# State-space front of a decoder kernel: parts of delta cast on ScalarE, first two scan steps from 32-row products, stacked copies counted by quarter

## The chip, the cores and the metric

One NeuronCore of one Trainium2 chip runs the whole kernel. The metric is the device time of one launch in microseconds, the median of three runs. Smaller is better.

## The reference, cut to the stage that is touched

The program is a decoder of two layers over x of shape (2, 256, 128), with a context of (2, 512, 128). The change is in the first block, a gated selective state-space model (the first 74 us or so); two cross-attentions, a self-attention and two expert feed-forward blocks follow it. What the block computes:

```python
def _selective_ssm(x, dt_w, dt_b, Bp_w, Bp_b, Cp_w, Cp_b, A_log, D_p):
    delta = jax.nn.softplus(x @ dt_w + dt_b)
    Bt = x @ Bp_w + Bp_b
    Ct = x @ Cp_w + Cp_b
    A = -jnp.exp(A_log)                       # (128, 16)
    def step(h, inp):
        xt, dt, bt, ct = inp
        dA = jnp.exp(dt[..., None] * A)
        dBx = dt[..., None] * bt[:, None, :] * xt[..., None]
        h = dA * h + dBx
        y = jnp.einsum('bdn,bn->bd', h, ct)
        return (h, y)
...
xn = _ln(x, ln1_g, ln1_b); xm = _ln(xn, ln_g, ln_b)
x1 = xm @ w1_w + w1_b
xc = silu(conv1d(x1, conv_w, width 3, per channel))
y = _selective_ssm(xc, ...)
v = silu(xm @ v1_w + v1_b)
x = (y * v) @ w2_w + w2_b + res
```

The matmul and convolution lines of the second half are abridged; the first function is as it stands.

## The kernel before, in words

Five engine programs (TensorE, VectorE, ScalarE, GpSimd and SyncE, which issues all DMAs) are written out by hand, each in a fixed order, and meet at semaphores. Nothing is scheduled by a tool: an engine runs its instructions in the order of the code, and an instruction whose semaphore has not come holds back all behind it.

**The front.** Two norms on VectorE (with GpSimd for the reciprocal roots), four transposes on TensorE, the projections w1 and v1, the convolution on VectorE, two Silu on ScalarE (`gate`, then `xc`), then three projections of `xc` into PSUM banks 3, 4 and 5: dt, B and C. delta is softplus: ScalarE does Abs, Exp and Ln into `dtmp`, VectorE puts it together as `dl[:, 0]` (L960). ScalarE also forms `nA` = -exp(A_log) (L662, L664), and copies B and C out of PSUM (L673, L675) and the normed context `cxnT` (L641, two of them). A change of function set on ScalarE costs a table load, which stands as a row of its own; `set_table` (L647) is a one-column activation that draws the load to its place.

**The spread.** The scan runs with 128 lanes that hold 8 channels by 16 states, so there are 16 scan steps `s`, each over all 512 tokens. Step s needs eight channels of delta, each repeated over 16 lanes, and the same of delta times xc (called dx). The repetition is a matmul with a 0/1 selector `sel_g`. To keep float32 accuracy from bf16 products, delta and dx are each split into three bf16 parts (`dparts`, three parts of each of the two kinds): part 0 is the cast, part 1 the cast of the rest, part 2 what is then left. A product sums the three parts at once, because they are stacked on 96 rows in `quads[32 * part + row, kind, q]`, where q = 0 to 3 is the quarter of 32 channels. Moving a part to its row group crosses partitions. For q = 0 ScalarE does it for delta (three copies, L684) and VectorE for dx (three copies, L971); for q = 1, 2 and 3 SyncE issues 18 DMAs from SBUF to SBUF (L445), each of 32 KB. `ORDER` gives quarter and index of each step: (0,0), (0,1), (1,0), (1,1), (2,0), (3,0), (2,1), (3,1), and then (q, 2) and (q, 3) for all four q.

**A scan step.** TensorE spreads delta into bank s % 2 and dx into bank 2 + s % 2; ScalarE does exp(scale * delta) with the scale from `nA` into `dA` (L708); VectorE multiplies the dx bank by B (L978) and scans (L983); GpSimd multiplies by C (L544). Beside each step TensorE does four products of the value projection of the next attention (`values0`), and ScalarE copies those out (L699). TensorE may write the banks of step s when `dA_done` and `scan_done` have reached s - 1. Step 2 waits for the six copies of q = 1 (`second_quads`), step 4 for the twelve copies of q = 2 and 3 together (`late_quads`).

## Time and profile before

| | |
|---|---|
| median of 3 runs | 488.54 us (488.38 to 488.86) |
| profiled execution, its own time | 487.24 us |
| its span (first to last instruction) | 485.1 us |
| TensorE busy, of the span | 423.2 us, 87% |
| VectorE / ScalarE / GpSimd busy | 306.9 / 206.8 / 145.0 us |
| mean granted TensorE clock | 0.976 of full |
| first scan step's multiply (L978) | starts at 32.09 us |
| last scan ends | about 63.6 us |

The profile is of one execution; its times count from the span's start. A busy share says little here, since the stages have different limits: the front is a chain through four engines, the scan stage is VectorE's, the rest is mostly TensorE's. So what a change in the front is worth is read from the chain of the front and from what each scan step waited for.

### The profile page before, as it was taken

The numbers are of one execution on the slowest core, as the hardware profiler recorded it, in microseconds if no ns is written. First come the engines' busy times: TensorE is split into PE (matmuls) and PEld (weight loads), VectorE is DVE, ScalarE is ACT, GpSimd is POOL, SyncE is SP. The second block draws the span as 40 slices with busy tenths as digits, with TensorE's granted clock in tenths as the row PEclk, the third lists the DMA queues.
The fourth block names the chain that finished last, engine by engine and source line by source line (L and its number), as shares of the span: only waits on it lengthen the run. The fifth ranks groups of instructions, "written<-read, shape, count | busy, mean of one in ns | idle before, by whom it ended". The sixth has DMA issues, their size and how long they took to land.

```text
span 485.1 us, 7466 instructions
## 1 busy us (share of the span) xinstructions
PE 423.2 (87%) x2852; PEld 269.4 (56%) x2860; DVE 306.9 (63%) x712; ACT 206.8 (43%) x268; POOL 145.0 (30%) x138
## 2 busy tenths in 40 slices
PE   5867989999999999789999878698578999997984
PEld 5665645444555556556778355344434445556874
DVE  4789976676666665416213587953697777338754
ACT  1765623333333322153323388574154445546320
POOL 3226647877777774100302200000200000005111
PEclk9989999999999999999999887999998999999998
DMA  8611000000023110610440430000000000010000
GB/s 306 263 34 59 1 0 2 1 1 1 0 84 134 45 45 0 219 51 1 110 59 17 62 40 3 3 3 1 0 1 3 1 3 1 2 34 1 1 1 22
DMA packets 7791, 19.58 MB, mean 40 GB/s; under 512 B 1862, under 2 KB 3686, under 8 KB 7238
## 3 DMA queue, kind: packets, MB, share of 16 engines
q1 hardware_dynamic: 7756, 19.10, 13.5%
q8 instruction: 23, 0.38, 0.3%
q14 instruction: 12, 0.10, 0.1%
HBM read 17.26 MB, written 1.15 MB: 38 GB/s over the span
## 4 chain that ended last, share of the span: by engine, by line
PE 60%; DVE 21%; ACT 5%; issue 5%; POOL 5%; SPq 2%; DMA 1%; DVEq 0%; POOLq 0%
PE ps L1373 58%; DVE ps L1170 3%; DVE mx_a L1174 2%; POOL big L588 2%; SPq L445 1%; ACT big L768 1%; DVE big L983 1%; DVE ps L978 1%; POOL rstd L521 1%; PE ps L1385 1%; POOL big L595 1%; PE ps L1753 1%; DMA ident<-in_ident 1%; DVE big L1332 1%; DVE attn_w L917 1%
## 5 line engine op out<-in xcount | busy, mean ns | idle before, releaser
L1373 PE MATMUL ps<-big,late 128*32 128x256 f32 (+4 forms) x792 | 99.8, 383 | 11.8 <-DVE mid L909 4.5
L1373 PEld LDWEIGHTS ps<-big,late 128*32 128x32 f32 (+3 forms) x800 | 38.9, 117 | 52.0 <-issue 22.0
L794 ACT ACTIVATE big<-ps 128x1024 f32<-128x1024 f32 x48 | 48.9, 1023 | 40.3 <-PE ps L1373 39.8
L1373 PE MATMUL ps<-late,big 128*128 128x128 f32 (+1 forms) x448 | 64.1, 275 | 1.6 <-DVE mx_x L1170 1.3
L519 POOL TENSOR_SCALAR vareps<-meanvar 128x4 f32<-128x4 f32 (+2 forms) x11 | 2.6, 232 | 197.4 <-DVE meanvar L886 193.7
L732 ACT ACTIVATE big<-ps 128x1024 f32<-128x1024 f32 x32 | 32.8, 1024 | 65.3 <-PE ps L1373 58.9
L1373 PEld LDWEIGHTS ps<-late,big 128*128 128x128 f32 (+1 forms) x448 | 44.7, 152 | 25.2 <-issue 21.0
L588 POOL TENSOR_TENSOR big<-big 128x512 f32<-128x512 f32 x32 | 41.0, 1283 | 28.2 <-DVE big L1055 28.2
L1170 DVE CUSTOM_DVE_ANT_0 ps<-ps,big 128x512 f32<-128x512 f32 x64 | 42.6, 717 | 10.0 <-PE ps L1373 6.9
L1055 DVE TENSOR_SCALAR big<-big 128x1024 f32<-128x1024 f32 x32 | 27.6, 864 | 33.3 <-ACT big L732 33.3
L1373 PE MATMUL ps<-ident 128*128 128x128 f32 x232 | 30.3, 293 | 5.7 <-DMA ident<-in_ident 5.7
L1373 PEld LDWEIGHTS ps<-ident 128*128 128x128 f32 x232 | 29.5, 209 | 6.8 <-DMA ident<-in_ident 5.7
L1373 PE MATMUL ps<-ctx_r,attn_w 128*128 128x512 f32 x64 | 32.6, 619 | 0.7 <-ACT late L699 0.7
L753 ACT ACTIVATE big<-ps 128x512 f32<-128x512 f32 x32 | 18.9, 597 | 29.0 <-PE ps L1373 29.0
L1373 PE MATMUL ps<-attn_w,big 128*128 128x128 f32 x192 | 25.9, 281 | 6.0 <-DVE big L1332 3.7
L1373 PE MATMUL ps<-xT,late 128*128 128x512 f32 x64 | 29.0, 596 | 1.2 <-ACT big L753 1.2
L1373 PEld LDWEIGHTS ps<-attn_w,big 128*128 128x128 f32 x192 | 23.4, 192 | 10.0 <-DVE big L1332 5.3
L1046 DVE RECIPROCAL big<-ps 128x256 f32<-128x256 f32 x16 | 28.0, 1748 | 1.3 <-PE ps L1373 1.3
L1096 DVE SCALAR_TENSOR_TENSOR summed<-ps,g,summed 128x128 f32<-128x128 f32 x28 | 7.9, 344 | 31.5 <-PE ps L1373 31.5
L1373 PE MATMUL ps<-big,mid 64*128 64x256 f32 x192 | 27.2, 403 | 0.0
L1373 PE MATMUL ps<-xT,attn_w 128*128 128x256 f32 (+1 forms) x80 | 24.8, 433 | 0.9 <-ACT xT L641 0.9
L544 POOL TENSOR_TENSOR big<-big,mid 128x512 f32<-128x512 f32 x16 | 20.4, 1272 | 16.2 <-DVE big L983 16.2
(255 smaller groups left out, 691.8 us busy)
## 6 DMA issues: line engine op xcount, KB each, us to landing
attn_w<-in_w_x SPq DMA_DIRECT2D x1, 2560.0 KB, 13.1
big<-parts_kx SPq DMA_DIRECT2D x18, 128.0 KB
late<-in_w_up SPq DMA_DIRECT2D x1, 2048.0 KB, 8.9
late<-in_w_dn SPq DMA_DIRECT2D x4, 512.0 KB, 3.9
attn_w<-in_w_up SPq DMA_DIRECT2D x1, 1024.0 KB, 5.9
attn_w<-in_w_dn SPq DMA_DIRECT2D x1, 1024.0 KB, 7.9
parts_kx<-ctx_r SPq DMA_DIRECT2D x1, 768.0 KB, 3.3
rowv<-in_rowv SPq DMA_DIRECT2D x1, 576.0 KB, 4.1
```

The lines of the kernel that those rows point to most:

```text
L445: sp.dma_start(quads[32 * i:32 * i + 32, kind, q, :], dparts[32 * q:32 * q + 32, kind, i, :]).then_inc(S["second_quads" if q == 1 else "la ...
L544: nc.gpsimd.tensor_tensor(hC[:, s % 8, :], hs[:, s % 4, :], Cn[:], ALU.mult).then_inc(S["hC_done"], 1)
L588: nc.gpsimd.tensor_tensor(esum[:, s, :].rearrange("p (r t) -> p r t", r=2), e[:, :, 0, :], e[:, :, 1, :], ALU.add).then_inc(S["e0_sum"], 1)
L732: nc.scalar.activation(ex[:, n % 3, :].rearrange("p (r n) -> p r n", r=2), ps[:, 2 * (n % 2):2 * (n % 2) + 2, :], ACT.Exp).then_inc(S["e0_ ...
L753: nc.scalar.activation(eh0[:, e % 2, c, :], ps[:, n % 3, :], ACT.Gelu).then_inc(S["up0_act"], 1)
L794: nc.scalar.activation(ex1[:, n % 3, :].rearrange("p (r n) -> p r n", r=2), ps[:, 2 * (n % 2):2 * (n % 2) + 2, :], ACT.Exp, scale=scale).t ...
L1046: link(nc.vector.reciprocal(dst, ps[:, 4 + b, T:2 * T]))
L1055: nc.vector.tensor_scalar(ex[:, n % 3, :], ex[:, n % 3, :], float(np.exp(CLIP)), float(np.exp(-CLIP)), ALU.min, ALU.max).then_inc(S["e0_cl ...
L1096: ins = nc.vector.scalar_tensor_tensor(summed[:, j, :], ps[:, 5 + e % 2, j * D:(j + 1) * D], g0[:, 3, j, e:e + 1], summed[:, j, :] if e el ...
L1170: nc.vector.tensor_tensor_reduce(ps[:, bank, :], ps[:, bank, :], mq[:, 2 * b + q, :], 1.0, -FAR, ALU.add, ALU.max, dst).then_inc(S[f"{L}_r ...
L1174: nc.vector.tensor_reduce(dst, ps[:, bank, :].rearrange("p (h k) -> p h k", h=heads), AX.X, ALU.max).then_inc(S[f"{L}_redmax"], 1)
L1373: return nc.tensor.matmul(o, lhsT, rhs, start=start, stop=stop, skip_group_check=shared)
```

## The change

Five things are done, all in the front of the first block:

- `nA` is made at the very start of ScalarE's program, in place of the one-column Identity. Where it stood, ahead of Abs, there is now a `set_table(ACT.Exp)`.
- Parts 0 and 1 of delta are cast by ScalarE (behind the copy of B and the copy of C), part 2 is subtracted by VectorE, not GpSimd. VectorE computes dx before it starts on the rests. ScalarE's table load for Exp and the two `cxnT` copies now come behind the second cast.
- The six copies for q = 0 ahead of step 0 (L684, L971) are gone. Steps 0 and 1 take each part straight from `dparts[0:32]` by a product of 32 rows, three of them accumulated in PSUM (`first_spread`): twelve products in the place of four. `values0(0, 0)` and `values0(0, 1)` both stand behind them.
- SyncE now issues 24 copies, in the order of the list `QUADS`; q = 0, which is needed from step 8 on, comes last.
- Each quarter has a semaphore: steps 2, 4, 5 and 8 wait for q = 1, 2, 3 and 0, with six copies each.

Some semaphores were renamed or merged (`rope_signed`, `x_scr` and `ones_rows`), with the same waits in effect. The diff, without the lists of semaphores and that renaming:

```diff
@@ -321,6 +321,13 @@
+        QUADS = ([(0, 0, 1), (0, 0, 2), (0, 0, 3), (0, 1, 1), (1, 0, 1), (0, 2, 1), (1, 1, 1), (1, 2, 1)]
+                 + [(0, 1, 2), (0, 2, 2)] + [(1, i, 2) for i in range(PARTS)]
+                 + [(0, 1, 3), (0, 2, 3)] + [(1, i, 3) for i in range(PARTS)]
+                 + [(kind, i, 0) for kind in range(2) for i in range(PARTS)])
...
+        QUAD_SEMS = ("first_quads", "second_quads", "late_quads", "third_quads")
...
@@ -438,13 +445,10 @@
-            for q in (1, 2, 3):
-                for kind, parts in enumerate(("delta_parts", "dx_parts")):
-                    for i in range(PARTS):
-                        sp.wait_ge(S[parts], i + 1)
-                        sp.dma_start(quads[32 * i:32 * i + 32, kind, q, :],
-                                     dparts[32 * q:32 * q + 32, kind, i, :]
-                                     ).then_inc(S["second_quads" if q == 1 else "late_quads"], 16)
+            for kind, i, q in QUADS:
+                sp.wait_ge(S["dx_parts" if kind else "delta_parts"], i + 1)
+                sp.dma_start(quads[32 * i:32 * i + 32, kind, q, :], dparts[32 * q:32 * q + 32, kind, i, :]
+                             ).then_inc(S[QUAD_SEMS[q]], 16)
...
@@ -529,10 +533,6 @@
-            pool.wait_ge(S["delta_parts"], 2)
-            nc.gpsimd.tensor_tensor(dparts[:, 0, 2, :], dtmp[:, 0, :], dparts[:, 0, 1, :], ALU.subtract
-                                    ).then_inc(S["delta_parts"], 1)
...
@@ -648,7 +648,9 @@
             act.wait_ge(consts, 1)
-            set_table(ACT.Identity)
+            link(nc.scalar.activation(nA[:, 0, :], vec[:, VEC["A_log"][0]:VEC["A_log"][0] + NG],
+                                      ACT.Exp))
+            link(nc.scalar.mul(nA[:, 1, :], nA[:, 0, :], -1.0))
             to_cols(xT[:], 0, "xT_ps", "xT_done", v("ln_g"), v("ln_b"), 1)
...
@@ -659,9 +661,7 @@
             nc.scalar.activation(xc[:], cv[:, 0, :], ACT.Silu).then_inc(S["xc_done"], 1)
-            link(nc.scalar.activation(nA[:, 0, :], vec[:, VEC["A_log"][0]:VEC["A_log"][0] + NG],
-                                      ACT.Exp))
-            link(nc.scalar.mul(nA[:, 1, :], nA[:, 0, :], -1.0))
+            set_table(ACT.Exp)
             act.wait_ge(S["dt_ps"], 1)
...
@@ -672,18 +672,17 @@
                                  ).then_inc(S["BC_done"], 1)
+            act.wait_ge(S["delta_done"], 1)
+            nc.scalar.activation(dparts[:, 0, 0, :], dl[:, 0, :], ACT.Copy).then_inc(S["delta_parts"], 1)
             nc.scalar.activation(Cn[:], ps[:, 5, :], ACT.Identity, bias=v("Cp_b")
...
+            act.wait_ge(S["delta_rest"], 1)
+            nc.scalar.activation(dparts[:, 0, 1, :], dtmp[:, 0, :], ACT.Copy
+                                 ).then_inc(S["delta_parts"], 1)
+            set_table(ACT.Exp)
             for i in range(2):
...
                         v("ctx_g"), v("ctx_b"), i + 1)
-            set_table(ACT.Exp)
-            act.wait_ge(S["delta_parts"], PARTS)
-            for i in range(PARTS):
-                ins = nc.scalar.activation(quads[32 * i:32 * i + 32, 0, 0, :], dparts[0:32, 0, i, :],
-                                           ACT.Copy)
-            ins.then_inc(S["delta_quads"], 1)
...
@@ -951,25 +950,30 @@
             dve.wait_ge(S["lg_done"], 1)
-            link(nc.vector.scalar_tensor_tensor(dl[:, 0, :], cv[:, 1, :], 0.0, dtmp[:, 2, :],
-                                                ALU.max, ALU.add))
-            nc.vector.tensor_copy(dparts[:, 0, 0, :], dl[:, 0, :]).then_inc(S["delta_parts"], 1)
-            dve.wait_ge(S["delta_parts"], 1)
-            link(nc.vector.tensor_tensor(dtmp[:, 0, :], dl[:, 0, :], dparts[:, 0, 0, :], ALU.subtract))
-            nc.vector.tensor_copy(dparts[:, 0, 1, :], dtmp[:, 0, :]).then_inc(S["delta_parts"], 1)
+            nc.vector.scalar_tensor_tensor(dl[:, 0, :], cv[:, 1, :], 0.0, dtmp[:, 2, :],
+                                           ALU.max, ALU.add).then_inc(S["delta_done"], 1)
+            dve.wait_ge(S["delta_done"], 1)
             dve.wait_ge(S["xc_done"], 1)
             link(nc.vector.tensor_tensor(dl[:, 1, :], dl[:, 0, :], xc[:], ALU.mult))
-            split(dl[:, 1, :], [dparts[:, 1, i, :] for i in range(3)], dtmp[:, 1, :], S["dx_parts"])
-            dve.wait_ge(S["dx_parts"], PARTS)
-            for i in range(PARTS):
-                ins = nc.vector.tensor_copy(quads[32 * i:32 * i + 32, 1, 0, :], dparts[0:32, 1, i, :])
-            ins.then_inc(S["dx_quads"], 1)
+            dve.wait_ge(S["delta_parts"], 1)
+            nc.vector.tensor_tensor(dtmp[:, 0, :], dl[:, 0, :], dparts[:, 0, 0, :], ALU.subtract
+                                    ).then_inc(S["delta_rest"], 1)
+            nc.vector.tensor_copy(dparts[:, 1, 0, :], dl[:, 1, :]).then_inc(S["dx_parts"], 1)
+            dve.wait_ge(S["dx_parts"], 1)
+            link(nc.vector.tensor_tensor(dtmp[:, 1, :], dl[:, 1, :], dparts[:, 1, 0, :], ALU.subtract))
+            dve.wait_ge(S["delta_parts"], 2)
+            dve.wait_ge(S["delta_rest"], 1)
+            nc.vector.tensor_tensor(dparts[:, 0, 2, :], dtmp[:, 0, :], dparts[:, 0, 1, :], ALU.subtract
+                                    ).then_inc(S["delta_parts"], 1)
+            nc.vector.tensor_copy(dparts[:, 1, 1, :], dtmp[:, 1, :]).then_inc(S["dx_parts"], 1)
+            dve.wait_ge(S["dx_parts"], 2)
+            nc.vector.tensor_tensor(dparts[:, 1, 2, :], dtmp[:, 1, :], dparts[:, 1, 1, :], ALU.subtract
+                                    ).then_inc(S["dx_parts"], 1)
...
@@ -1412,7 +1416,6 @@
             pe.wait_ge(ld["sel"], 32)
-            pe.wait_ge(S["delta_parts"], PARTS)
             pe.wait_ge(S["gate_done"], 1)
...
@@ -1443,28 +1446,34 @@
+            def first_spread(kind, s):
...
+                for part in range(PARTS):
+                    pe.wait_ge(S[("delta_parts", "dx_parts")[kind]], part + 1)
+                    ins = mm(ps[:, 2 * kind + s, :], sel_g[0:32, ORDER[s][1], :],
+                             dparts[0:32, kind, part, :], part == 0, part == PARTS - 1)
+                ins.then_inc(S[("spread_d", "spread_x")[kind]], 1)
...
+            first_spread(0, 0)
+            first_spread(0, 1)
+            first_spread(1, 0)
+            first_spread(1, 1)
+            pe.wait_ge(ld["x0"], 16)
+            pe.wait_ge(S["cxnT_done"], 2)
+            values0(0, 0)
+            values0(0, 1)
             for s, (q, i) in enumerate(ORDER):
-                if s >= 2:
-                    pe.wait_ge(S["dA_done"], s - 1)
-                if s == 0:
-                    pe.wait_ge(S["delta_quads"], 1)
-                elif s == 2:
-                    pe.wait_ge(S["second_quads"], 16 * 2 * PARTS)
-                elif s == 4:
-                    pe.wait_ge(S["late_quads"], 16 * 4 * PARTS)
+                if s < 2:
+                    continue
+                pe.wait_ge(S["dA_done"], s - 1)
+                if s in (2, 4, 5, 8):
+                    pe.wait_ge(S[QUAD_SEMS[q]], 16 * 2 * PARTS)
                 mm(ps[:, s % 2, :], sel_g[:, i, :], quads[:, 0, q, :]).then_inc(S["spread_d"], 1)
-                if s == 0:
-                    pe.wait_ge(S["dx_quads"], 1)
-                if s >= 2:
-                    pe.wait_ge(S["scan_done"], s - 1)
+                pe.wait_ge(S["scan_done"], s - 1)
                 mm(ps[:, 2 + s % 2, :], sel_g[:, i, :], quads[:, 1, q, :]
...
                     y_of((7, 9, 14).index(s))
-                if s == 0:
...
-                    pe.wait_ge(ld["x0"], 16)
-                    pe.wait_ge(S["cxnT_done"], 2)
                 values0(s // 2, s % 2)
```

**From Ln to the first scan steps, on ScalarE and VectorE.** ScalarE before: the first row is the Ln (L670), `mid` written from `ps` is B and C, `ctx_r` is `cxnT`, L684 the copies into `quads`, L708 the exponent of steps 0 and 1.

```order
L670 ACTIVATE dtmp<-dtmp 128x512 [waits act_own]
L673 ACTIVATE mid<-ps,vec 128x512 [waits BC_ps]
L675 ACTIVATE mid<-ps,vec 128x512
L641 ACTIVATE ctx_r<-ps,vec 128x512 [waits cxnT_ps] x2
L647 ACT_TABLE_LOAD
L647 ACTIVATE act_table<-neghalf 128x1
L684 ACTIVATE big<-mid 32x512 [waits delta_parts]
L684 ACTIVATE big<-mid 32x512 x2
L708 ACTIVATE big<-ps,nA 128x2x255 [waits spread_d] x2
```

ScalarE now, from the same Ln; L676 and L680 are the casts of delta's parts, L707 the exponent.

```order
L670 ACTIVATE dtmp<-dtmp 128x512 [waits act_own]
L673 ACTIVATE mid<-ps,vec 128x512 [waits BC_ps]
L676 ACTIVATE mid<-mid 128x512 [waits delta_done]
L677 ACTIVATE mid<-ps,vec 128x512
L680 ACTIVATE mid<-dtmp 128x512 [waits delta_rest]
L647 ACT_TABLE_LOAD
L647 ACTIVATE act_table<-neghalf 128x1
L641 ACTIVATE ctx_r<-ps,vec 128x512 [waits cxnT_ps] x2
L707 ACTIVATE big<-ps,nA 128x2x255 [waits spread_d] x2
```

Two casts of 128 partitions have come in, each behind a wait on VectorE, the three copies of 32 partitions are gone, and table load and `cxnT` copies have moved behind the second cast.

VectorE before, from delta (L960) to the multiply of step 0 (L978); L902 to L911 are the split of dx.

```order
L960 SCALAR_TENSOR_TENSOR mid<-cv,dtmp 128x512 [waits lg_done,dve_own]
L962 CAST mid<-mid 128x512 [waits dve_own]
L964 TENSOR_TENSOR dtmp<-mid 128x512 [waits delta_parts]
L965 CAST mid<-dtmp 128x512 [waits dve_own]
L967 TENSOR_TENSOR mid<-mid 128x512 [waits xc_done]
L902 CAST mid<-mid 128x512 [waits dve_own]
L904 TENSOR_TENSOR dtmp<-mid 128x512 [waits dx_parts]
L909 CAST mid<-dtmp 128x512 [waits dve_own]
L911 TENSOR_TENSOR mid<-dtmp,mid 128x512 [waits dx_parts]
L971 COPY big<-mid 32x512 [waits dx_parts]
L971 COPY big<-mid 32x512 x2
L978 TENSOR_TENSOR ps<-ps,mid 128x512 [waits spread_x,BC_done]
```

VectorE now, from delta (L958) to the multiply of step 0 (L982).

```order
L958 SCALAR_TENSOR_TENSOR mid<-cv,dtmp 128x512 [waits lg_done,dve_own]
L962 TENSOR_TENSOR mid<-mid 128x512 [waits xc_done,delta_done]
L964 TENSOR_TENSOR dtmp<-mid 128x512 [waits delta_parts,dve_own]
L966 CAST mid<-mid 128x512
L968 TENSOR_TENSOR dtmp<-mid 128x512 [waits dx_parts]
L971 TENSOR_TENSOR mid<-dtmp,mid 128x512 [waits delta_rest,delta_parts,dve_own]
L973 CAST mid<-dtmp 128x512
L975 TENSOR_TENSOR mid<-dtmp,mid 128x512 [waits dx_parts]
L982 TENSOR_TENSOR ps<-ps,mid 128x512 [waits spread_x,BC_done]
```

Two casts and three copies have left VectorE, one subtraction (L971 now) has come in, and two instructions wait for ScalarE's casts (`delta_parts`).

**The first steps on TensorE.** Before, from the idle products on `ident` to step 2; `big,sel` is a spread, `attn_w,ctx_r` is `values0`.

```order
L1373 MATMUL ps<-ident 128x128 x20
L1373 MATMUL ps<-big,sel 128x512 [waits gate_done,delta_quads,delta_parts,loaded_sel]
L1373 MATMUL ps<-big,sel 128x512 [waits dx_quads]
L1373 MATMUL ps<-attn_w,ctx_r 128x128 [waits cxnT_done,loaded_x0]
L1373 MATMUL ps<-attn_w,ctx_r 128x128 x3
L1373 MATMUL ps<-big,sel 128x512 x2
L1373 MATMUL ps<-attn_w,ctx_r 128x128 x4
L1373 MATMUL ps<-big,sel 128x512 [waits second_quads,dA_done]
L1373 MATMUL ps<-big,sel 128x512 [waits scan_done]
```

Now; `mid,sel` is a product of 32 rows, straight from a part.

```order
L1377 MATMUL ps<-ident 128x128 x20
L1377 MATMUL ps<-mid,sel 128x512 [waits delta_parts,gate_done,loaded_sel]
L1377 MATMUL ps<-mid,sel 128x512 [waits delta_parts] x5
L1377 MATMUL ps<-mid,sel 128x512 [waits dx_parts] x6
L1377 MATMUL ps<-attn_w,ctx_r 128x128 [waits cxnT_done,loaded_x0]
L1377 MATMUL ps<-attn_w,ctx_r 128x128 x7
L1377 MATMUL ps<-big,sel 128x512 [waits second_quads,dA_done]
L1377 MATMUL ps<-big,sel 128x512 [waits scan_done]
```

Twelve products stand where four did, and all eight of `values0` for the first two steps stand behind them.

**SyncE's copies**, before and then now, from the last input load (L438, now L445) to the load of `cxT`.

```order
L438 DMA eb<-in_eb 128x32
L445 DMA big<-mid 32x512 [waits delta_parts] x3
L445 DMA big<-mid 32x512 [waits dx_parts] x3
L445 DMA big<-mid 32x512 [waits delta_parts] x3
L445 DMA big<-mid 32x512 [waits dx_parts] x3
L445 DMA big<-mid 32x512 [waits delta_parts] x3
L445 DMA big<-mid 32x512 [waits dx_parts] x3
L460 DMA ctx_r<-in_cxT 128x1024 [waits cxnT_ps]
```

```order
L445 DMA eb<-in_eb 128x32
L450 DMA big<-mid 32x512 [waits delta_parts] x4
L450 DMA big<-mid 32x512 [waits dx_parts]
L450 DMA big<-mid 32x512 [waits delta_parts]
L450 DMA big<-mid 32x512 [waits dx_parts] x2
L450 DMA big<-mid 32x512 [waits delta_parts] x2
L450 DMA big<-mid 32x512 [waits dx_parts] x3
L450 DMA big<-mid 32x512 [waits delta_parts] x2
L450 DMA big<-mid 32x512 [waits dx_parts] x3
L450 DMA big<-mid 32x512 [waits delta_parts] x3
L450 DMA big<-mid 32x512 [waits dx_parts] x3
L464 DMA ctx_r<-in_cxT 128x1024 [waits cxnT_ps]
```

The first copies of dx stood behind one of delta's third part and came three in a row; now copies of delta's first part for all of q = 1, 2 and 3 lead, and six more stand at the end.

## Rows read from the trace of the kernel before

**Rows 1.** The page, part 4: the chain that ended last, share by engine.

```profile
PE 60%; DVE 21%; ACT 5%; issue 5%; POOL 5%; SPq 2%; DMA 1%; DVEq 0%; POOLq 0%
```

**Rows 2.** The chain in order of time: start us, us, what (SPq is SyncE's queue).

```profile
30.66 0.51 SPq L445
...
37.54 0.59 SPq L445
38.13 0.04 issue
38.17 1.83 DMA big<-mid
```

**Rows 3.** Timeline of VectorE: start us, us, engine, line, operation, tiles, shapes, count, idle before.

```profile
24.48 0.69 DVE L960 SCALAR_TENSOR_TENSOR mid<-cv,dtmp 128x512 f32<-128x512 f32 x1 [1.45 <-ACT dtmp L670]
25.21 0.43 DVE L962 CAST mid<-mid 128x512 bf16<-128x512 f32 x1
25.67 0.69 DVE L964 TENSOR_TENSOR dtmp<-mid 128x512 f32<-128x512 f32 x1
...
27.46 1.26 DVE L902 CAST mid<-mid 128x512 bf16<-128x512 f32 x1
...
30.66 0.87 DVE L971 COPY big<-mid 32x512 bf16<-32x512 bf16 x3
32.09 0.70 DVE L978 TENSOR_TENSOR ps<-ps,mid 128x512 f32<-128x512 f32 x1 [0.56 <-PE ps L1373]
32.83 1.22 DVE L983 TENSOR_TENSOR_SCAN big<-big,ps 128x512 f32<-128x512 f32 x1
34.44 0.70 DVE L978 TENSOR_TENSOR ps<-ps,mid 128x512 f32<-128x512 f32 x1 [0.40 <-PE ps L1373]
...
40.77 0.70 DVE L978 TENSOR_TENSOR ps<-ps,mid 128x512 f32<-128x512 f32 x1 [0.65 <-PE ps L1373]
...
42.64 0.67 DVE L978 TENSOR_TENSOR ps<-ps,mid 128x512 f32<-128x512 f32 x1
...
46.33 0.68 DVE L978 TENSOR_TENSOR ps<-ps,mid 128x512 f32<-128x512 f32 x1
```

**Rows 4.** Timeline of ScalarE, from the table load behind `xc` on.

```profile
19.29 1.28 ACT L662 ACT_TABLE_LOAD   x1
20.59 0.22 ACT L662 ACTIVATE nA<-vec 128x16 f32<-128x16 f32 x1
...
21.08 0.69 ACT L666 ACTIVATE dtmp<-ps,vec 128x512 f32<-128x512 f32 x1
...
23.75 0.63 ACT L670 ACTIVATE dtmp<-dtmp 128x512 f32<-128x512 f32 x1
...
25.42 1.45 ACT L641 ACTIVATE ctx_r<-ps,vec 128x512 f32<-128x512 f32 x2
...
28.46 1.91 ACT L684 ACTIVATE big<-mid 32x512 bf16<-32x512 bf16 x3
```

**Rows 5.** Timeline of GpSimd: the subtraction for delta's third part.

```profile
26.90 1.53 POOL L534 TENSOR_TENSOR mid<-dtmp,mid 128x512 bf16<-128x512 f32 x1 [4.59 <-DVE mid L965]
```

**Rows 6.** Timeline of TensorE: PE is the product, PEld its weight load.

```profile
22.88 4.63 PE L1373 MATMUL ps<-ident 128*128 128x128 f32 x40
30.52 0.38 PE L1373 MATMUL ps<-big,sel 96*128 96x512 bf16 x1 [3.00 <-ACT big L684]
...
31.82 1.73 PE L1373 MATMUL ps<-attn_w,ctx_r 128*128 128x128 f32 x8
...
35.57 0.21 PEld L1373 LDWEIGHTS ps<-big,sel 96*128 96x128 bf16 x2
35.68 0.60 PE L1373 MATMUL ps<-big,sel 96*128 96x512 bf16 x2
...
36.12 1.06 PE L1373 MATMUL ps<-attn_w,ctx_r 128*128 128x128 f32 x8
```

**Rows 7.** Windows: stretch, length, busy us by engine, granted clock, DMA share, GB/s.

```profile
33.00:34.00 1.00, 1.00 (x5) 0.66 (x5) 1.00 (x1) 0.00 (x0) 0.00 (x0) 0.50 0.25 66
288.40:291.80 3.40, 2.88 (x12) 1.47 (x12) 2.13 (x8) 3.30 (x6) 0.00 (x0) 0.50 0.00 0
```

19 lines of the change are left out of this document (9 added, 10 removed).

## The prediction, made before the changed kernel had run

> **What bounds the kernel now.** I first read the chain that ended last by engine: 60% of it is TensorE, 21% VectorE, 5% ScalarE, 2% SyncE's queue [rows 1]. So the kernel as a whole is a TensorE kernel, but a chain's share says nothing of the stage that is touched. I therefore read the chain in order of time over that stage. It runs through ScalarE (Silu, the two operations for `nA`, Abs, Exp, Ln), then through VectorE's splits, and at 30.66 it jumps to SyncE: twelve copies in a row, the last issued at 37.54, then 1.83 us of transfer until 40.00 [rows 2]. Only then can step 4 be spread. The reader should see two things: the end of the front is the queue of copies, and that queue could not go on before the first part of dx, and then ran issue after issue.
>
> Then the timeline of VectorE. Its multiplies of the scan steps start at 32.09, 34.44, then (step 4) 40.77, 42.64 (step 5) and 46.33 (step 7) [rows 3]. From step 4 to 7 that is (46.33 - 40.77) / 3 = 1.85 us a step, VectorE being busy all the time. From step 0 to 4 it is 8.68 us where four such steps are 7.41: 1.27 us of waiting, of which 2.35 - 1.85 = 0.50 lie behind step 0 and the other 0.77 ahead of step 4. Behind step 0 TensorE is slow: its clock is granted at 0.50 in the stretch from 33 to 34, so at 1.2 GHz [rows 7], and eight records of `values0` take 1.73 us where they take 1.06 four microseconds later [rows 6]. Before that TensorE had ended its idle products at 27.51 and had nothing until 30.52 [rows 6].
>
> **The change, part by part.** Times are those of the profiled execution.
>
> *Table and exponent.* Between the table load at 19.29 and Abs at 21.08 stand the two operations for `nA`; the first starts at 20.59, so both cost 0.49 [rows 4]. One small activation, about 0.22 like the first of them, takes their place: 0.27 saved. Abs, Exp, Ln and delta come 0.27 earlier, since ScalarE runs them without a gap. The two operations at the program's start cost nothing: they lie in the wait for the first transposes. There are as many table loads as before. Delta, which ended at 24.48 + 0.69 = 25.17 [rows 3], ends at 24.90.
>
> *Casts on ScalarE.* A cast on VectorE takes 0.43 [rows 3]; ScalarE takes 0.63 for a float32 tile of 128x512 in SBUF [rows 4]. The first cast runs from 24.94 to 25.57, about the 25.64 at which it ended before. It costs 0.2 more and gives the 0.27 back. VectorE does dx meanwhile (0.69), to 25.61, so it hardly waits.
>
> *VectorE up to the last part of dx.* From 25.67, with ScalarE's signal some 0.1 behind: four subtractions at 0.69 and two casts at 0.43 make 3.62, so 29.25. The cast of 27.46 took 1.26 instead of 0.43, beside GpSimd's subtraction from 26.90 to 28.43 [rows 3, 5]; I take it that this 0.83 goes with the GpSimd instruction, as no other lies there. If it stays, the last part comes at 30.1. Before, it came just ahead of the three copies at 30.66, which took 0.87 more [rows 3].
>
> *Twelve products of 32 rows.* A product of 96 rows takes 0.38, a pair 0.60, so each further one costs 0.22 [rows 6]. The trace has none of 32 rows. Bounds: 0.22 from the pair, and 0.44, twice that, were the clock at half. I take 0.22, as rows streamed (512) are what is alike. Delta's third part comes at about 28.15; from there stand seven products up to the one that closes dx of step 0: it starts at 28.22 + 6 x 0.22 = 29.54, behind the last part at 29.25, and ends at 29.92. The multiply of step 0 starts at 29.95, not 32.09: **2.14 us earlier**. At 0.44 each it would be 6 x 0.22 = 1.3 us later, still ahead of before.
>
> The weight loads of a pair overlap it: two of 0.21 in all from 35.57, the products from 35.68 on at 0.22 apart [rows 6], in the same rows of the array. The Trainium skill (TensorE: Matmul & The Clock Gate, The mechanism) says that a load overlaps a running product only where the two use other row groups, and here all twelve use the same. By that rule each of the six gaps ahead of step 0 grows by the load's 0.10, and the first multiply comes 0.6 later, at 30.55, and with the 0.3 that the copies below leave free the time would be 485.7; the trace does not agree for 96 rows.
>
> *ScalarE's second cast, table load, `cxnT`.* The rest of delta is there at 26.36, the cast ends at 27.02, the load 1.28 later, the small activation brings 28.54, the two `cxnT` copies (1.45) 29.97 [rows 4]. The three copies of 1.91 are gone [rows 4]. So the exponent of step 0 runs from 30.0 to 30.7, and the scan of step 0 can start at 30.73, not 32.83 [rows 3]. ScalarE and TensorE arrive within 0.1 us: whichever slips delays the start.
>
> *Steps 1 to 3.* If TensorE has work from 28.2 on, I expect its clock to stay at 2.4 GHz: its gap is then 27.51 to 28.2, not 3 us. `values0` for both steps ends at about 30.2 + 2 x 1.06 = 32.4. Step 2 also needs q = 1. That and step 3 then go at 1.85: **0.50 saved**. With the clock at half, both `values0` take 1.7 and this 0.5 stays.
>
> *The copies.* One issue takes (37.54 - 30.66) / 11 = 0.625 [rows 2]. The first starts at 25.62, as before, and each of the parts is there when its turn comes (the tightest, dx part 2 for the eighth, at 29.25 against 30.0). So the eighth lands at 25.62 + 8 x 0.625 + 1.83 = 32.45, the thirteenth at 35.6, the eighteenth at 38.7, the twenty-fourth at 42.4. Needed: step 2 at about 32.5 (free until 33.2), step 4 at 36.8, step 8 at about 44.6, all met. Step 5's multiply would start at 29.95 + 5 x 1.85 = 39.2; from 38.7 on it needs 0.14 to start and 0.60 for the pair [rows 2, 6], so 39.5. The 0.77 ahead of step 4 goes, **a new wait of 0.3 ahead of step 5 comes**: step 5 stands at 39.5 instead of 42.64, **3.1 us earlier**. SyncE's load of `cxT` behind the copies is used only in layer 1.
>
> Sum: 2.14 + 0.50 + 0.77 - 0.3 = 3.1 us. It has a ceiling of its own: the queue starts when it did before, so a faster front would buy nothing more, and up to 0.3 us of slip there costs nothing. Steps 5 to 15 are VectorE's at 1.85 and wait only for work of their own stage. Behind them the chain is TensorE's, and nothing there waits for a load of the start. I let the 3.1 through whole. The profiled execution would be 487.24 - 3.1 = 484.1 (its span 482.0); it is 1.3 below the median of the runs, and I predict against that: 488.54 - 3.1 = **485.4 us**.
>
> **The rivals.**
>
> *A. The start slips.* Products of 32 rows at 0.44, a half-rate clock in steps 0 to 3, or the 0.83 of the cast staying: each costs 0.5 to 1.0 beyond the slack, together 1.5 at most. Gain 1.6 to 2.6, time 486.0 to 486.9. For it: TensorE now works in thin groups between waits. Against: before, it had been idle for 3 us ahead of the clock's fall [rows 6, 7], and that gap goes. Chance 0.16.
>
> *B. The gain is given back later.* Something behind the scans does not move. For it: over nine tenths of the time are made behind the front. Against: every wait there is on another engine's work, and the chain has no absolute point. Gain under 1, time about 488. Chance 0.07.
>
> *C. Slower.* Later on TensorE's clock is at half in the stretch from 288.4 to 291.8 while it is busy 2.88 of 3.40 us [rows 7]; half of such a stretch, up to 1.7 us, is lost. The clock falls behind waits of TensorE, and the waits stand elsewhere in time if everything shifts by 3 us. The price passes the gain from two further such stretches on (3.4 against 3.1) and is felt as slower with three: 488.54 - 3.1 + 5.1 = 490.5. Against: the three runs of before lie within 0.5 us, so no such thing comes and goes there. Chance 0.05.
>
> *D. More than thought,* 3.8 or more (484.7 or less), if one of the later stretches at half rate vanishes: 1.7 more, 483.7. Chance 0.06.
>
> **How the numbers follow.** The forecast, a gain of 2.6 to 3.7, has 0.66. The range reaches from 484.0 (most of D out) to 487.0, the end of A; B and C are outside, with 0.12, and half of D. 0.2% of this kernel, 1.0 us, is about what a measurement can tell from none: forecast, A and D are faster (0.88), B is the same (0.07), C slower (0.05).
>
> **What would show it.** Right: Abs at about 20.8; two casts of 0.63 on ScalarE; no cast on VectorE over 0.5; step 0's multiply at 29.9 to 30.1 and step 1's 1.85 behind; the clock at 1.00 from 28 to 36; the eighteenth copy landed at 38.7 and step 5's multiply at 39.5 with a wait of 0.3 for it; after that the same intervals as before. Wrong: a start later than 30.6, steps over 1.85 apart among the first four, a copy's landing over 2 us, or a later interval that is longer than before by what the front has gained.

## The result, and the profile after

The changed kernel takes **485.51 us** (median of 21 runs, 483.55 to 490.45); the kernel before, run beside it, 488.77 us (21 runs, 486.98 to 496.43). The ratio is 0.9947, with a 95% interval of 0.9925 to 0.9968, so 2.6 us less, give or take 1.1. The run of 496.43 us is a slow one and is left out of the ratio. The prediction was 485.4 us, range 484.0 to 487.0. The profiled execution of the changed kernel took 486.05 us with a span of 484.2, against 487.24 and 485.1 in the kernel before.

The chain that ended last, by engine, for [rows 1]: SyncE's queue has gone from 2% to 0%.

```profile
PE 63%; DVE 21%; issue 5%; POOL 5%; ACT 4%; DMA 1%; SPq 0%; DVEq 0%; POOLq 0%; ACTq 0%
```

ScalarE's timeline in the changed kernel, for [rows 4]: Abs follows the small activation by 0.11 us, and two casts of 0.63 us stand where VectorE had them.

```profile
18.41 0.63 ACT L663 ACTIVATE mid<-cv 128x512 f32<-128x512 f32 x1 [0.23 <-DVE cv L944]
19.06 1.28 ACT L647 ACT_TABLE_LOAD   x1
20.35 0.20 ACT L647 ACTIVATE act_table<-neghalf 128x1 f32<-128x1 f32 x1
20.46 0.67 ACT L666 ACTIVATE dtmp<-ps,vec 128x512 f32<-128x512 f32 x1
...
24.57 0.63 ACT L676 ACTIVATE mid<-mid 128x512 bf16<-128x512 f32 x1 [0.26 <-DVE mid L958]
...
26.03 0.63 ACT L680 ACTIVATE mid<-dtmp 128x512 bf16<-128x512 f32 x1 [0.25 <-DVE dtmp L964]
...
29.41 1.25 ACT L707 ACTIVATE big<-ps,nA 128x510 f32<-128x510 f32 x2
```

VectorE's timeline, for [rows 3]. The multiplies of the scan's steps are the L982 rows.

```profile
23.85 0.69 DVE L958 SCALAR_TENSOR_TENSOR mid<-cv,dtmp 128x512 f32<-128x512 f32 x1 [1.44 <-ACT dtmp L670]
24.57 0.69 DVE L962 TENSOR_TENSOR mid<-mid 128x512 f32<-128x512 f32 x1
...
25.91 0.42 DVE L966 CAST mid<-mid 128x512 bf16<-128x512 f32 x1
...
28.16 0.69 DVE L975 TENSOR_TENSOR mid<-dtmp,mid 128x512 bf16<-128x512 f32 x1
29.63 0.70 DVE L982 TENSOR_TENSOR ps<-ps,mid 128x512 f32<-128x512 f32 x1 [0.78 <-PE ps L1377]
...
31.50 0.67 DVE L982 TENSOR_TENSOR ps<-ps,mid 128x512 f32<-128x512 f32 x1
...
33.99 0.70 DVE L982 TENSOR_TENSOR ps<-ps,mid 128x512 f32<-128x512 f32 x1 [0.56 <-PE ps L1377]
...
35.86 0.67 DVE L982 TENSOR_TENSOR ps<-ps,mid 128x512 f32<-128x512 f32 x1
...
37.71 0.68 DVE L982 TENSOR_TENSOR ps<-ps,mid 128x512 f32<-128x512 f32 x1
...
39.56 0.68 DVE L982 TENSOR_TENSOR ps<-ps,mid 128x512 f32<-128x512 f32 x1
```

And step 3's multiply in the kernel before, which [rows 3] leaves out:

```profile
38.19 0.67 DVE L978 TENSOR_TENSOR ps<-ps,mid 128x512 f32<-128x512 f32 x1
```

TensorE's timeline and windows (stretch, length, busy us of PE, PEld, DVE, ACT and POOL, granted clock, DMA share, GB/s), for [rows 6, 7], and SyncE's queue.

```profile
22.65 4.63 PE L1377 MATMUL ps<-ident 128*128 128x128 f32 x40
27.21 2.96 PE L1377 MATMUL ps<-mid,sel 32*128 32x512 bf16 x12
30.10 3.00 PE L1377 MATMUL ps<-attn_w,ctx_r 128*128 128x128 f32 x16
32.89 1.06 PE L1377 MATMUL ps<-big,sel 96*128 96x512 bf16 x2
...
37.99 0.59 PE L1377 MATMUL ps<-big,sel 96*128 96x512 bf16 x2 [0.21 <-DMA big<-mid]
```

```profile
30.00:31.00 1.00, 1.00 (x9) 0.90 (x9) 0.97 (x2) 0.67 (x2) 0.00 (x0) 0.99 0.16 42
31.00:34.00 3.00, 3.00 (x15) 2.57 (x14) 2.40 (x4) 1.03 (x2) 1.76 (x2) 0.50 0.19 52
...
195.00:198.00 3.00, 3.00 (x9) 1.97 (x9) 1.71 (x7) 0.07 (x1) 0.00 (x0) 0.50 0.26 68
```

```profile
25.23 15.18 SPq L450 DMA_DIRECT2D big<-mid  x24
```

Step 5's multiply stands at 39.56 instead of 42.64: **3.08 us earlier**. By its parts, each the interval of [rows 3] less that of the rows above: 0.24 because the whole front began earlier in this execution (Silu of `xc` at 18.41); 0.39 between that Silu and the end of delta; 1.83 from the end of delta to the first multiply (5.09 instead of 6.92); 0.48 between steps 0 and 1 (1.87, was 2.35); 0.73 between steps 3 and 4 (37.71 - 35.86, was 40.77 - 38.19); 0.02 between 4 and 5. **And 0.61 lost** between steps 1 and 2: 2.49 where 1.88 was, under a granted clock of 0.50. Together 3.08.

The last scan ends at 60.54, 3.08 before that of the kernel before (63.62). From there to the last instruction the changed kernel's profiled execution takes 2.2 us more. The reader sees where by the start of GpSimd's first operation of each norm (`vareps`), before and after: 200.80 and 198.32, then 267.18 and 265.78, and 481.26 and 480.25 at the end. So 0.60 of the lead is lost up to the first of these norms, 1.08 up to the second and 0.39 behind it. Around the first norm lies a stretch at half rate, from 194.8 to 198.2, that the trace of the kernel before does not have. (It has one from 363.1 to 366.5 that the changed kernel's lacks, and there no lead is won: the interval between the norms on both sides of it is 80.76 us before and 80.75 after.) So this one execution keeps 1.2 of the 3.1 us, and only the medians show the 3.

### The profile page after: what moved, and what is told of

It is laid out like the page before. It is cut to its first block, busy times and chain, and to the rows that moved or that the text cites. A ratio compares the mean times of both kernels' runs of the same rounds, so it can differ in the third digit from the quotient of the medians.

```text
span 484.2 us, 7494 instructions
## 1 busy us (share of the span) xinstructions
PE 426.3 (88%) x2868; PEld 270.2 (56%) x2868; DVE 304.9 (63%) x708; ACT 206.0 (43%) x267; POOL 143.4 (30%) x137
## 4 chain that ended last, share of the span: by engine, by line
PE 63%; DVE 21%; issue 5%; POOL 5%; ACT 4%; DMA 1%; SPq 0%; DVEq 0%; POOLq 0%; ACTq 0%
PE ps L1377 61%; DVE ps L1174 3%; DVE mx_a L1178 2%; DVE big L987 2%; POOL big L588 2%; ACT big L767 1%; DVE ps L982 1%; PE ps L1389 1%; POOL rstd L525 1%; DVE big L1059 1%; POOL big L595 1%; PE ps L1762 1%; DMA ident<-in_ident 1%; DVE big L1336 1%; DVE big L1050 1%
## 5 line engine op out<-in xcount | busy, mean ns | idle before, releaser
L1377 PE MATMUL ps<-big,late 128*32 128x256 f32 (+4 forms) x800 | 101.0, 382 | 11.4 <-DVE mid L908 4.9
L1377 PE MATMUL ps<-xT,attn_w 128*128 128x256 f32 (+1 forms) x80 | 24.8, 433 | 0.9 <-ACT xT L641 0.9
```

The costliest lines, as they stand in the source:

```text
L1377: return nc.tensor.matmul(o, lhsT, rhs, start=start, stop=stop, skip_group_check=shared)
```

## The experiments

Positions in the front are compared from the end of delta, since one execution's front starts later than another's: the Silu of `xc` starts between 18.36 and 19.51. Where several runs are named, the time is their median, and the ratio is that of this kernel to the kernel before on the same chip.

**Copies alone.** The kernel before, with the new order of its 18 copies and own counts by quarter (q = 0 still by ScalarE and VectorE):

```
-for q in (1, 2, 3): for kind, ...: for i in range(PARTS): sp.dma_start(...)
+for kind, i, q in QUADS:            # the changed kernel's order, without q = 0
-elif s == 4: pe.wait_ge(S["late_quads"], 16 * 4 * PARTS)
+elif s in (4, 5): pe.wait_ge(S[QUAD_SEMS[q]], 16 * 2 * PARTS)
```

> The kernel before with one part of the change: the 18 copies in the new order, and steps 2, 4 and 5 each waiting for its own quarter. Front, casts and the copies of q = 0 as before. My sum puts 0.77 us to this part (the wait ahead of step 4): step 0's multiply stays at 32.1, step 5's comes at 41.9 instead of 42.64, time some 0.8 us under the kernel before, ratio 0.9985. Rival (the copies gave most of it, since the queue was the chain's last link): step 5 at 40 and 2 us or more. Rival (all of the gain is the earlier start): no change, step 4 waits as before.

Measured: 488.27 us (10 runs), ratio 0.9999 [0.998, 1.0019]. VectorE's multiplies of steps 3, 4 and 5:

```profile
38.23 0.68 DVE L980 TENSOR_TENSOR ps<-ps,mid 128x512 f32<-128x512 f32 x1
...
40.08 0.68 DVE L980 TENSOR_TENSOR ps<-ps,mid 128x512 f32<-128x512 f32 x1
...
41.93 0.68 DVE L980 TENSOR_TENSOR ps<-ps,mid 128x512 f32<-128x512 f32 x1
```

The wait ahead of step 4 is gone: step 4 follows step 3 by 1.85 instead of 2.58, 0.73 less, for 0.77 predicted. From the end of delta, step 5 comes only 0.42 earlier (17.04 instead of 17.46), because here the clock fell to half at 31.1 and not at 32.0: the first multiply comes 7.14 after delta (6.92 before) and step 1 follows by 2.49 (2.35). The whole time shows no gain; 0.7 us is inside the interval of plus or minus 0.9.

**The wait for both quarters put back** into the changed kernel (step 4 waits for q = 2 and q = 3):

```
-if s in (2, 4, 5, 8): pe.wait_ge(S[QUAD_SEMS[q]], 16 * 2 * PARTS)
+if s in (2, 4, 8):    pe.wait_ge(S[QUAD_SEMS[q]], 16 * 2 * PARTS)
+if s == 4:            pe.wait_ge(S[QUAD_SEMS[3]], 16 * 2 * PARTS)
```

> The changed kernel, but step 4 waits for the copies of q = 2 and of q = 3, as before the change. By my account of the queue the eighteenth copy lands at about 37.85, so step 4's multiply comes at 38.6 instead of 37.71 and step 5's at 40.45 instead of 39.56: 0.9 us of the gain is lost, time about 486.4. Rival (the queue is no limit, counting by quarter did nothing): step 4 and the time unchanged.

Measured: 488.04 us (10 runs), ratio 0.9994 [0.9977, 1.001]. TensorE waits ahead of step 4's pair:

```profile
39.09 0.59 PE L1377 MATMUL ps<-big,sel 96*128 96x512 bf16 x2 [1.55 <-DMA big<-mid]
```

The last scan ends 36.93 us after delta, 36.00 in the changed kernel: 0.93 for the wait, or 0.67 against the changed kernel's second trace below (36.26). The median is 2.5 above the changed kernel's, which was not run beside it; 0.7 to 0.9 of it is this wait, the rest was not located. Both edits to the copies together say that the count by quarter is worth 0.7 to 0.9 us in the front.

**Delta's third part on GpSimd again:**

```
-nc.vector.tensor_tensor(dparts[:, 0, 2, :], dtmp[:, 0, :], dparts[:, 0, 1, :], ALU.subtract)
+nc.gpsimd.tensor_tensor(dparts[:, 0, 2, :], dtmp[:, 0, :], dparts[:, 0, 1, :], ALU.subtract)
```

> The changed kernel with the subtraction for delta's third part on GpSimd again. If VectorE's cast is stretched by GpSimd's instruction, one cast of VectorE between 26.7 and 28.3 takes about 1.26 us instead of 0.42 and delta's third part comes 0.5 later: step 0's multiply at 30.1 instead of 29.63, time 0 to 0.5 us over the changed kernel. Rival (the 1.26 of before was a property of that cast, not of GpSimd): no cast over 0.5, VectorE 0.69 shorter, step 0 no later than 29.7.

Measured: 486.81 us (10 runs), ratio 0.9982 [0.996, 1.0004]. VectorE, and GpSimd's one instruction:

```profile
26.29 0.42 DVE L971 CAST mid<-mid 128x512 bf16<-128x512 f32 x1
26.75 0.69 DVE L973 TENSOR_TENSOR dtmp<-mid 128x512 f32<-128x512 f32 x1
27.48 1.26 DVE L974 CAST mid<-dtmp 128x512 bf16<-128x512 f32 x1
```

```profile
27.18 1.27 POOL L539 TENSOR_TENSOR mid<-dtmp,mid 128x512 bf16<-128x512 f32 x1 [4.72 <-ACT mid L685]
```

The cast that lies beside GpSimd's subtraction takes 1.26, the one ahead of it 0.42; the subtraction on VectorE at 26.75, also partly beside it, keeps its 0.69. The prediction's reading of [rows 3, 5] holds. The first multiply comes 5.38 after delta instead of 5.09: 0.29 later, as delta's third part is (GpSimd ends at 28.45, 3.53 after delta; VectorE's subtraction in the changed kernel ended 3.24 after it). It is no more than that because VectorE is spared the subtraction. The clock stayed full in this trace, and the last scan ends 35.61 after delta, earlier than in the changed kernel (36.00).

**The stack of q = 0 instead of 32-row products** (three copies on ScalarE and three on VectorE, four products of 96 rows, 18 DMAs, all else as changed):

```
-first_spread(0, 0); first_spread(0, 1); first_spread(1, 0); first_spread(1, 1)
+pe.wait_ge(S["delta_parts"], PARTS + 1)
+for s in range(2): mm(ps[:, s, :], sel_g[:, s, :], quads[:, 0, 0, :])
+... (the same for dx), and the six copies into quads[:, :, 0] as before
```

> The changed kernel, but steps 0 and 1 by stacked products of 96 rows: ScalarE (three copies, 1.9 us, ahead of the cxnT copies) and VectorE (three copies, 0.87) fill q = 0, and SyncE issues 18 copies. My account: exponent of step 0 at 31.3 instead of 29.4, scan of step 0 at 32.0 instead of 30.36, step 5's multiply at 40.7 to 41.0 instead of 39.56, time 1.1 to 1.5 us over the changed kernel. Rival (the queue of copies alone sets step 5, and the products of 32 rows bring nothing): step 5 at 39.6 and the time of the changed kernel.

Measured: 487.89 us (10 runs), ratio 0.9985 [0.9965, 1.0006]. TensorE and VectorE:

```profile
30.22 1.86 PE L1386 MATMUL ps<-big,sel 96*128 96x512 bf16 x4 [2.84 <-ACT big L684]
28.98 0.87 DVE L984 COPY big<-mid 32x512 bf16<-32x512 bf16 x3
31.77 0.70 DVE L991 TENSOR_TENSOR ps<-ps,mid 128x512 f32<-128x512 f32 x1 [1.91 <-PE ps L1386]
```

The first multiply comes 7.13 after delta, 2.04 later than with the 32-row products; as the steps behind it then go at 1.85 without a gap, the last scan ends 1.36 later. Step 0's scan starts at 32.50, for 32.0 expected: the granted clock is 0.50 from 29.9 on, behind TensorE's wait of 2.84 us, and the four products take 1.86 us where 0.38 + 3 x 0.22 = 1.04 would do. By an estimate, 0.6 to 0.7 of the 2.04 is this half rate. Without it the multiply would come about 6.5 after delta, only 0.4 earlier than in the kernel before (6.92), although the casts are on ScalarE: TensorE waits for ScalarE's three copies, so the parts of the change do not simply add. The 32-row products are the largest of them.

**The changed kernel a second time:**

> The changed kernel once more, beside the next three. Its first trace had the clock at half from 31.0 to 34.4, step 2's multiply 2.49 behind step 1's, and step 5's multiply 15.0 us behind the end of delta. If that half-rate stretch belongs to the kernel, it stands here again at the same place; if it comes and goes by execution, step 2 may follow at 1.85 and step 5 come at 14.4 to 14.6. Time 485 to 486.

Measured: 485.71 us (11 runs), ratio 0.994 [0.9921, 0.9958]. Delta's end to the first multiply is 5.09 again, and the half rate is there again: the sixteen records of `values0` take 3.68 us. It is not at quite the same place: it lasts from 30.3 to 33.7, not from 31.0 to 34.4, while the twelve products stand 0.15 later. So step 2 follows step 1 by 2.75 and step 5 comes 15.28 after delta, not 15.02.

```profile
27.36 2.96 PE L1377 MATMUL ps<-mid,sel 32*128 32x512 bf16 x12
30.25 3.68 PE L1377 MATMUL ps<-attn_w,ctx_r 128*128 128x128 f32 x16
```

**The same twelve products with 128 rows.** The selector is padded with zeros, so each product also reads the other quarters and adds zero times them; start and length of the products stay.

```
-mm(..., sel_g[0:32, ORDER[s][1], :], dparts[0:32, kind, part, :], ...)
+mm(..., sel_p[:, ORDER[s][1], :],    dparts[:, kind, part, :], ...)   # sel_p: 0 from row 32 on
```

> The changed kernel, its twelve first products over 128 rows: the selector is padded with zero rows (an extra input of 64 KB), so the result is the same and only the number of rows in TensorE's array changes. If products of 32 rows count as little work and that is why the clock fell at 31.0, the clock stays at 1.00 from 28 to 36 here, step 2 follows step 1 at 1.85, and step 5's multiply comes 14.4 us behind the end of delta (15.0 in the changed kernel); time 0.6 less. Rival (the fall has another cause, such as the short waits between the products, or comes by execution): half rate from about 31 again and step 5 at 15.0. The spacing of the products is 0.22 either way.

Measured: 486.23 us (10 runs), ratio 0.9962 [0.9935, 0.999]. TensorE and the window that stands at 0.50 in the changed kernel:

```profile
27.25 3.07 PE L1379 MATMUL ps<-mid,sel_p 128*128 128x512 bf16 x12
30.16 1.95 PE L1379 MATMUL ps<-attn_w,ctx_r 128*128 128x128 f32 x16
```

```profile
31.00:34.00 3.00, 3.00 (x24) 2.44 (x24) 2.97 (x4) 2.08 (x4) 1.61 (x2) 1.00 0.21 55
```

All steps go at 1.85; step 5 comes 14.35 after delta instead of 15.02, and the last scan ends 35.34 after it instead of 36.00. The whole time is not lower. The chain of this kernel ahead of step 5 (start, length, what) shows the queue at the edge: TensorE waits for the eighteenth copy, 1.41 us; VectorE does not.

```profile
35.53 0.59 SPq L452
36.12 0.04 issue
36.16 1.88 DMA big<-mid
38.04 0.14 issue
38.17 0.39 PE ps L1379
```

**Fewer, larger copies** (delta and dx of q = 2, 3 and 0 in one DMA of 64 KB: 15 copies), on the changed kernel and on the 128-row one:

```
-QUADS = (... + [(0, 1, 2), (0, 2, 2)] + [(1, i, 2) ...] + ... + [(kind, i, 0) ...])
+QUADS = ([(0,0,1), (0,1,1), (1,0,1), (0,2,1), (1,1,1), (1,2,1)] + [(2, i, q) for q in (2, 3, 0) ...])
```

> The changed kernel with delta and dx of one part in one copy of 64 KB for q = 2, 3 and 0: 12 copies ahead of step 5 instead of 18. If the queue sets step 5 (my prediction's 0.3 of new wait), the wait goes and step 5 comes up to 0.3 earlier. If, as the changed kernel's trace shows, step 5 was late from TensorE's half rate at step 2 and not from the queue, nothing moves: step 5's multiply 15.0 behind the end of delta with the half rate, 14.4 without. A paired copy's issue should take 0.6 like a single one, or up to 1.2 if it goes by rows.

> Both of these edits. Without the half rate and without the queue nothing is left between the steps: step 5's multiply 14.35 behind the end of delta, all first eight steps at 1.85, end of the last scan 0.65 earlier than in the changed kernel, time 0.6 less. If one of the two limits is imaginary, this is no faster than the kernel with the other edit alone.

Measured: 485.74 us (5 runs), ratio 0.9938 [0.991, 0.9965], step 5 15.28 after delta; and 486.24 us (12 runs), ratio 0.9957 [0.9936, 0.9978], step 5 14.36 after delta, as in the 128-row kernel (14.35). Against the changed kernel's second trace, 15.28 is no loss by the copies: both have the half rate at the same place. The queue took 10.75 us for 15 copies, not 15.18 for 24, and nothing came earlier: it does not yet bound the front.

**Two parts undone, one execution each.** Delta's casts back on VectorE, and A's exponent back behind `xc`:

```
-nc.scalar.activation(dparts[:, 0, 0, :], dl[:, 0, :], ACT.Copy)      # and the one for part 1
+nc.vector.tensor_copy(dparts[:, 0, 0, :], dl[:, 0, :])               # and the one for part 1
```

```
-nA = exp, mul ahead of the first norm; set_table(ACT.Exp) behind xc
+set_table(ACT.Identity) ahead of the first norm; nA = exp, mul behind xc
```

> The changed kernel with delta's two bf16 casts back on VectorE and none on ScalarE; all else as changed. Theory (the front's gain is VectorE's own chain getting shorter by what ScalarE takes over): VectorE's row from the dx product to the last part has no wait in the changed kernel, so two casts of 0.42 push step 0's multiply from 5.09 us after the end of delta to 5.93, and every later step by the same: last scan 36.84 us after the end of delta instead of 36.0. Rival (the twelve products of TensorE set the start, and they could begin earlier on VectorE's casts): step 0's multiply no more than 5.4 us after delta. The whole time: nothing is claimed from one execution.

> The changed kernel with A's exponent and its negation back behind the second Silu, and the Identity table asked for at the start as before. Theory: the start of the Abs stands 2.43 us behind the start of the Silu of xc in the kernel before and 2.05 in the changed one, so this kernel goes back to 2.43: the end of delta 6.51 us after that Silu's start instead of 6.13 (0.38 later), more than the 0.27 that the prediction gave the edit. Rival (the difference came from the input's arrival): 6.13, as in the changed kernel.

Measured: with the casts on VectorE the first multiply comes 5.89 after delta (31.18 - 25.29), 0.80 later than in the changed kernel, as the theory had it; the last scan ends 38.16 after delta, not 36.84, because the clock stood at half until 38 and step 2 came 3.77 behind step 1. With the late exponent delta ends 6.53 after the start of the Silu, 6.13 in the changed kernel: 0.40, for 0.38 expected. Its ScalarE:

```profile
20.40 0.21 ACT L662 ACTIVATE nA<-vec 128x16 f32<-128x16 f32 x1
20.65 0.22 ACT L664 ACTIVATE nA<-nA 128x16 f32<-128x16 f32 x1
20.90 0.69 ACT L666 ACTIVATE dtmp<-ps,vec 128x512 f32<-128x512 f32 x1
```

**TensorE's waits at 190 us filled** with idle products, on the changed kernel and on the 128-row one:

```
+idle_work(2, 7)
 denominators0(NPAIR - 1, 1)
+idle_work(2, 17)
 output0(NPAIR - 1)
```

> The changed kernel with 7 idle products of 128 columns ahead of the last sums of the first attention and 17 behind them, which fill TensorE's two waits at 190.5 and 192.1 us of the changed kernel's profile (0.99 and 2.32 us). Theory (the half-rate stretch at 194 to 199 us is the later part of a gain that was given back: it follows those two waits): granted clock 1.00 from 190 to 200 us, the norm behind the output product about 1.7 us earlier against the last scan, and 1 to 1.7 us off the whole time (484.0 to 484.7). Rival 1 (the stretches further on move with any shift): the stretch at 194 is gone but another place pays it back, time within 0.5 us of 485.7. Rival 2: the idle products are late and hold up the output product, time 486 or more.

> Both: the first two steps' products of 128 rows with a padded selector, and the idle products at 190 us. Theory: step 5's multiply 14.35 us after the end of delta, the last scan 0.9 us earlier than in the changed kernel, no half-rate stretch at 31 nor at 194, so 484 to 485 us: faster than both kernels. Rival (later half-rate stretches decide): no difference from the changed kernel, 485.7 within 0.7, although the first part is earlier.

Measured: 486.31 us (12 runs), ratio 0.996 [0.9938, 0.9983]; and 486.16 us (7 runs), ratio 0.9951 [0.993, 0.9971]. TensorE and windows of the first:

```profile
190.54 1.83 PE L1377 MATMUL ps<-ident 128*128 128x128 f32 x14
192.30 0.65 PE L1377 MATMUL ps<-big 128*64 128x256 f32 x4
192.88 4.06 PE L1377 MATMUL ps<-ident 128*128 128x128 f32 x34
196.78 1.06 PE L1377 MATMUL ps<-attn_w,big 128*128 128x128 f32 x8
```

```profile
192.00:195.00 3.00, 3.00 (x27) 2.50 (x26) 1.97 (x2) 0.00 (x0) 0.00 (x0) 1.00 0.55 186
195.00:198.00 3.00, 3.00 (x27) 2.87 (x26) 0.34 (x2) 0.00 (x0) 0.00 (x0) 1.00 0.00 1
```

The clock stays at 1.00. That the two waits let it fall without the filling is likely and not shown by this pair, since the 128-row kernel, unfilled, has the same two waits (0.99 and 2.32 us) and kept 1.00 from 190 to 200:

```profile
193.90 1.16 PE L1379 MATMUL ps<-attn_w,big 128*128 128x128 f32 x8 [2.32 <-DVE big L1053]
```

So did the kernel before and the one with the copies alone; the other nine unfilled traces have a stretch at half rate there. Over all runs the filled kernels have less time at half rate (median 18.4 and 16.5 us, 23.2 in the changed kernel; how it is read stands below). But the filling was mis-sized: one idle product is two records of TensorE, so 7 took 1.83 us where 0.99 were free and held the sums up by 0.7, and 17 took 4.06 where 2.32 were free: VectorE's sums were ready at 194.79 + 0.42 = 195.21, and the output product began at 196.78. The norm comes 139.28 us after the last scan, 137.78 in the changed kernel: 1.5 later, rival 2. A filling of the right length, about 3 and 9 products, was not run.

## Why the prediction came out right

**By its steps.** *Table and exponent:* 0.27 predicted, 0.39 in the trace and 0.40 with the edit undone. The small activation ends after the next one has begun, while the two operations for `nA` each waited for the other. *Casts on ScalarE:* right; the first ends 0.66 after delta, 0.67 predicted. Their worth in the front is the 0.80 that appears with them back on VectorE. *VectorE up to the last part of dx:* right; 4.31 after delta for 4.35, and the 0.83 of the long cast went with the GpSimd instruction. *Twelve products at 0.22:* right; (2.96 - 0.38) / 11 = 0.235 with what waits lie in it, and the multiply of step 0 stands 5.09 after delta for 5.05. The products of 32 rows with their weight loads in the same rows run as close as those of 96 (ten in 2.33 us with the late exponent: 0.22 apart), and those of 128 rows too (3.07 for twelve); the rule of the Trainium skill (TensorE: Matmul & The Clock Gate, The mechanism), by which the first multiply would be 0.6 later, is borne out in none of them. *Start of the scan:* right; the scan of step 0 begins 5.82 after delta, 5.83 predicted.

**The step that failed** is "I expect its clock to stay at 2.4 GHz" in steps 1 to 3. The 0.50 behind step 0 was saved, but between steps 1 and 2 the half rate cost 0.61. The prediction reasoned from the gap: without it no fall. The gap did go: TensorE's records stand side by side from 22.65 to 33 but for a gap of 0.03 us at 27.8, and the clock fell at 31.0 all the same. The prediction's own sign of being wrong, steps over 1.85 apart among the first four, came true, and so did a part of its rival A. What went ahead of the fall was no such wait but the twelve products of 32 rows.

Whether their rows are the cause is likely and not shown. For it: with 32 rows the clock fell in six of eight traces (the changed kernel twice, the wait for both quarters, paired copies, filled, casts on VectorE), with 128 rows in none of three, although these start their products at the same time (27.25 and 27.21) and take nearly the same length. Against it stands a rival, that the execution decides. The moment of the fall is not tied to the program: in the six it came 2.96 to 3.78 us after the first of the twelve products, 3.78 and 2.96 in the two executions of one kernel. Where it lies goes with the first rise of the clock, which is at 10.51 in the changed kernel's first trace (TensorE has 7 records a microsecond ahead of it, 11 behind): in all six, and in the three traces without such products that fell here (the kernel before, the copies alone, the stack), the fall came 20.48 us behind that rise. The same count in the traces that kept their clock leads to 4.44 (third part on GpSimd) and 2.33 us (late exponent) behind the first product, and with 128 rows to 4.60, 3.79 (with paired copies) and about 2.21 (filled). So the two escapes with 32 rows lie outside the stretch in which the others fell, and so do two of the three traces with 128 rows; only one of these, 3.79 against 3.78 in the changed kernel, sets the two widths side by side, and there the narrow one fell and the wide one did not.

**The new wait of 0.3** ahead of step 5 did not reach VectorE: TensorE waited 0.21, and step 5's multiply follows step 4's by 1.85. The term was a miscount. The prediction had the eighteenth copy landed at start + 18 x 0.625 + 1.83, but a landing counts from the start of a copy's issue and not from its end (in the chain of the 128-row kernel 1.88 us, from 36.16). [rows 2] shows it too: the copy that lands at 40.00 was issued at 38.17, one behind the 37.54 that the prediction called the last. So it is 17 issues: from 25.23 that makes 37.7 at 0.625, and TensorE's pair starts at 37.99. The other landings in the prediction were late by one issue too, which harmed none of them.

So two errors came close to cancelling. Of 3.11 predicted, 0.3 was not lost to the queue, 0.61 was lost to the clock, and the exponent gave 0.12 more; with 0.08 in the rounding of the other terms that is 2.84, and the 0.24 by which this execution started earlier, which is no part of the change, makes it 3.08.

**The copies** were otherwise right: the 0.77 ahead of step 4 went (0.73 here; 0.73 with the copies alone; 0.67 to 0.93 with the wait back). The ceiling was right in kind: by the trace of the 128-row kernel, "a faster front would buy nothing more" beyond another 0.3 us or so. There TensorE waits 1.41 us for the eighteenth copy, and its pair, from 38.17 to 38.76, is just in time for the multiply at 39.03. No faster front was run.

**From the front to the whole time.** "I let the 3.1 through whole": the medians say 3.3 (488.77 to 485.51) and 2.6 (488.35 to 485.71, second time); the profiled pair says 1.2. Both hold, because executions differ by what their later stretches at half rate are. Each run lists its mean granted clock c and span; 2 x (1 - c) x span is its time at half rate, 23.2 us for the changed kernel's profiled one. Over the 32 runs of the changed kernel the time rises by 0.29 us with each us of it (correlation 0.91; it ranges from 16 to 36 us). Rival C, whose mechanism this is, asked for three more stretches than before; in the profiled pair one came, at 194.8, behind TensorE's waits of 0.99 and 2.32 us at 190.5 and 192.1, and one went, at 363.1. The one that came cost most of the 2.2 us (0.60 and 1.08 around it), as much as the 1.7 that the prediction gave such a stretch. Its other reason against, that the three runs of before lay within 0.5 us, was luck of a small number: 21 runs spread by 2.9 us leaving the one of 496.43 out. In medians the changed kernel has 23.2 us at half rate and the kernel before 26.3 (76 runs beside the experiments; in 31 of them, on one chip, 23.3); in means 23.5 and 24.8. By that slope, 0.4 to 0.9 of the gain could be this and not the front. The runs do not tell it apart from chance. For the same reason the front's last 0.7 us (128 rows) shows in the trace and not in the median: no version that was run is shown to beat the changed kernel. That the medians came within 0.3 us of the forecast is in part luck: the front's two errors nearly cancelled, and by the slope above a later stretch like that from 194.8 to 198.2, more or less, moves a run by 1.0 (3.4 x 0.29).
